# First attention: the query clamp one group later, two masks earlier, and four row maxima moved to another place

## What is computed

```python
x = x + linear_attention(layernorm(x))          # 16 heads of 64, features exp(+f), exp(-f), causal
x = x + cross_attention(layernorm(x), ctx)      # 16 heads of 16, over 1024 context rows
x = x + experts(layernorm(x))                   # 8 experts, the best 2 of each row

def feature_map(t, K):
    f = einsum('hdf,bhld->bhlf', K, t)
    return maximum(concat([softmax(f), softmax(-f)]), 1e-12)
# linear attention: q, k, v = heads(x @ Wq), ...; qf, kf = feature maps
# o_l = sum_{m<=l} (qf_l . kf_m) v_m / (sum_{m<=l} qf_l . kf_m + 1e-12);  then o @ Wo
# cross attention: softmax(q k^T / 4) v, the row maximum subtracted before exp; then @ Wo
```

## Time and profile before

| | |
|---|---|
| time, median of 3 runs | 1252.89 us (1252.18 to 1253.55) |
| the profiled execution | 1252.72 us, its span 1250.9 us |
| busy share of the span | TensorE 92%, VectorE 76%, ScalarE 49%, GpSimd 29% |
| mean granted TensorE clock | 0.973 of full speed |
| first attention | from the start to about 555 us |
| from one L479 to the next over chunk 10 | 360.97 to 391.15 us |

### The profile page before, as it was taken

How to read it: one execution, slowest core, us unless ns; L and a number is a source line. 1 busy time by engine, 2 the same in 40 slices (tenths; PEclk the granted TensorE clock), 3 DMA queues, 4 the chain that set the end, 5 groups by cost and what they waited for, 6 DMA issues and landing times. The chain is left out here.

```text
span 1250.9 us, 29597 instructions
## 1 busy us (share of the span) xinstructions
PE 1147.8 (92%) x11658; PEld 682.9 (55%) x11659; DVE 953.1 (76%) x1758; ACT 610.1 (49%) x1151; POOL 365.3 (29%) x346
## 2 busy tenths in 40 slices
PE   7799899999899999979999999999999847999996
PEld 5566666676667766643344344334434334666665
DVE  6888868887888688778679777877889456677756
ACT  4332333334333333217678776776788722344443
POOL 3322255222522222112310320131100412566651
PEclk9899999999999999999999999999999977999998
DMA  8000025000400000013730480075050161111115
GB/s 255 27 1 2 2 54 104 1 2 1 79 1 2 1 2 1 2 55 58 136 69 9 77 177 4 8 129 102 2 207 2 52 180 41 60 63 63 63 58 204
DMA packets 61928, 73.64 MB, mean 59 GB/s; under 512 B 14336, under 2 KB 53376, under 8 KB 61168
## 3 DMA queue, kind: packets, MB, share of 16 engines
q1 hardware_dynamic: 58016, 61.56, 20.8%
q0 software_dynamic: 3792, 10.36, 2.6%
HBM read 52.86 MB, written 18.78 MB: 57 GB/s over the span
## 5 line engine op out<-in xcount | busy, mean ns | idle before, releaser
L1717 DVE TENSOR_REDUCE neg_max<-pS 128x1 f32<-128x1024 f32 x240 | 287.2, 1220 | 53.5 <-PE pS L1500 53.1
L1632 ACT ACTIVATE pt<-pR 128x512 f32<-128x512 f32 x512 | 286.5, 600 | 80.0 <-PE pR L1523 75.1
L1523 PE MATMUL pR<-qs,ks 100*32 100x512 bf16 x2048 | 190.7, 383 | 1.8 <-ACT pt L1632 1.6
L1500 PE MATMUL pS<-ks,qs 100*32 100x512 bf16 x1920 | 147.3, 382 | 6.0 <-DVE neg_max L1717 2.8
L1537 PE MATMUL b_pO<-pt,b_v 128*32 128x512 f32 x1024 | 135.2, 602 | 2.2 <-ACT pt L1632 1.6
L406 PE MATMUL pP<-w_feat,a_xT 128*128 128x512 f32 x244 | 117.7, 606 | 0.7 <-ACT w_feat L676 0.7
L298 POOL TENSOR_TENSOR kf<-kf,fsum 128x2048 f32<-128x2048 f32 (+1 forms) x17 | 58.1, 3421 | 185.6 <-DVE fsum L867 185.6
L1523 PEld LDWEIGHTS pR<-qs,ks 100*32 100x32 bf16 x2048 | 56.0, 96 | 95.3 <-issue 25.5
L298 POOL TENSOR_TENSOR qs<-qs,fsum 128x2048 f32<-128x2048 f32 (+1 forms) x17 | 58.5, 3446 | 143.4 <-DVE fsum L867 143.4
L1379 POOL COPY qs<-max_rows 3x512 bf16<-3x512 bf16 x60 | 36.7, 611 | 208.9 <-ACT max_rows L1625 205.9
L1500 PEld LDWEIGHTS pS<-ks,qs 100*32 100x32 bf16 x1920 | 51.4, 97 | 76.0 <-issue 35.8
(11 more groups left out here) (339 smaller groups left out, 2124.2 us busy)
## 6 DMA issues: line engine op xcount, KB each, us to landing
ks<-k_scr SPq DMA_DIRECT2D x8, 768.0 KB
qs<-q_scr SPq DMA_DIRECT2D x24, 256.0 KB
k_scr<-f SPq DMA_DIRECT2D x18, 256.0 KB, 2.6
ks<-k_scr SPq DMA_DIRECT2D x8, 512.0 KB
ks<-in_L_ffn_w_dram SPq DMA_DIRECT2D x2, 2048.0 KB, 10.5
ks<-in_L_ffn_w_dram SPq DMA_DIRECT2D x4, 1024.0 KB, 8.7
ks<-y_rows SPq DMA_DIRECT2D x16, 256.0 KB, 5.4
cx<-in_ctx_dram SPq DMA_DIRECT2D x3, 768.0 KB, 12.2
```

What stands on the lines that cost most here:

```text
L1500: ins = pe.matmul(pS1[q:q + XV, slot, 512 * half:512 * half + 512], qs[0:KR, bass.ds(par, 1), h, P * t + q:P * t + q + XV].rearrange("r a ...
L1523: ins = pe.matmul(ring[bank][q:q + XV, :], ks[0:KR, bass.ds(par, 1), h, P * j + q:P * j + q + XV].rearrange("r a n -> r (a n)"), qs[0:KR, ...
L1632: nc.scalar.activation(pt[:, j % 2, i, :], ring[bank], ACT.Exp).then_inc(exp_done, 1)
L1717: nc.vector.tensor_reduce(neg_max[:, hg % 2, u // G, u % G:u % G + 1], pS1[:, u % 2, :], AX_X, ALU.max, negate=True).then_inc(max_done, 1)
```

## The change

Six edits. In the first attention VectorE masks group g + 1 at the head of group g (before, the second query shift and the query sums came first), and clamps the queries of the next chunk in group 3, behind `normalise_o`, instead of in group 2. ScalarE copies the turned features of group 3 before the second query exponential. In chunk 15 `split_max` stands behind `normalise_o` of group 3 instead of ahead of it. Two units of the second head group (16 and 17 in the count of the first attention) are computed there: unit 16's scores before the last `o_transposes`, its maximum behind `split_max`; unit 17's scores inside the last `out_product`, its maximum behind `turned_maxima`. The cross attention starts with units 2 and 3, so that five units instead of seven are left for its opening. For this the table `neg_max` of both head groups is allocated outside the two functions.

```diff
         def unit_scores(u):
-            return pP if u < SOON or u % 2 == 0 else pDW
+            return pP if u < SOON or u % 2 == 0 or u >= NEW else pDW
...
                     for j in range(H // 2):
+                        if t == T - 1 and j == 2:
+                            token_scores(NEW + 1)
                         ins = pe.matmul(y_ps, oT[:, j, :], wo[:, j, :], start=(j == 0), stop=(j == H // 2 - 1))
...
-                    wait(pe, max_done, u if u < SOON else u - 1)
+                    wait(pe, max_done, u if u < SOON else u + 1 if u > NEW else u - 1)
+                    if u >= NEW:
+                        t, h = (u - NEW) // G, G + (u - NEW) % G
...
+                        if final:
+                            token_scores(NEW)
                         o_transposes(t)
...
                         prepare(prep, 2)
+                        prepare(prep, 3)
+                        f_copies(t, 3)
                         if has1:
                             exponentials(1, t + 1, 1, 1 - par)
-                        prepare(prep, 3)
-                        f_copies(t, 3)
...
                         for g in range(G):
+                            if final:
+                                for u in UNITS[g][:2]:
+                                    maximum(u)
+                            if g < G - 1:
+                                mask(t, g + 1)
                             if g == 1 and has1:
                                 shift(1, t + 1, 1, 1 - par, own)
                             if g == 2 and has1:
                                 denominators(1, t + 1, 1 - par, own)
                             if final:
-                                for u in UNITS[g][:2]:
-                                    maximum(u)
-                            if g < G - 1:
-                                mask(t, g + 1)
-                            if final:
                                 for u in UNITS[g][2:3]:
                                     maximum(u)
-                            if final and g == G - 1:
-                                split_max()
                             if g == 0 and has1:
                                 shift(1, t + 1, 0, 1 - par, own)
...
                             normalise_o(t, g, own)
+                            if final and g == G - 1:
+                                split_max()
+                                maximum(NEW)
                             if g == 0 and has2:
                                 normalise(t + 2)
-                            if g == 2 and has1:
+                            if g == G - 1 and has1:
                                 clamp(1, t + 1, 1 - par)
...
                         if final:
                             turned_maxima()
+                            maximum(NEW + 1)
...
-        AHEAD = 2
+        IN_LINEAR, AHEAD = 2, 4
...
-                    U = 16 * (G * b + hg - 1) + u
+                    U = 16 * (G * b + hg - 1) + u - IN_LINEAR
...
-                for u in range(AHEAD):
+                for u in range(IN_LINEAR, AHEAD):
                     scores_by_token(0, 1, u)
```

More of the change, by code:

```diff
@@ L62, in linear_attention @@
 def linear_attention(nc, x, Wq, Wk, Wv, Wo, Kq, Kk, xr, ctx_in, on, Cq, Ck, Cv, k_scr, q_scr, aug_scr,
-                     stats1, mv1, rstd1, q_scale, q_aug, ks, qs, v_first):
+                     stats1, mv1, rstd1, q_scale, q_aug, neg_max, ks, qs, v_first):
     with ExitStack() as ctx:
@@ L129, in linear_attention @@
         cv = ck_raw
-        neg_max = sb("a_neg_max", [P, TB, G])
         max_rest = sb("a_max_rest", [P, TB, G])
@@ L181, in linear_attention @@
         NEW, SOON = 16, 3
+        first_max = neg_max[:, 0]
         UNITS = [range(SOON, SOON + 4), range(SOON + 4, SOON + 8), range(SOON + 8, SOON + 12), range(SOON + 12, NEW)]
         def unit_scores(u):
-            return pP if u < SOON or u % 2 == 0 else pDW
+            return pP if u < SOON or u % 2 == 0 or u >= NEW else pDW
         def prepares(b, c):
@@ L957, in maximum @@
                     dve.wait_ge(s1_done, u + 1)
-                    nc.vector.tensor_reduce(neg_max[:, u // G, u % G:u % G + 1], unit_scores(u)[:, :],
+                    hg, n = u // NEW, u % NEW
+                    nc.vector.tensor_reduce(neg_max[:, hg, n // G, n % G:n % G + 1], unit_scores(u)[:, :],
                                             AX_X, ALU.max, negate=True).then_inc(max_done, 1)
@@ L964, in split_max @@
                     dve.wait_ge(s_k, 14)
-                    rows.did(nc.vector.tensor_copy(max_parts[:, :, :, 0], neg_max[:, :, :]))
+                    rows.did(nc.vector.tensor_copy(max_parts[:, :, :, 0], first_max))
                     rows.wait()
-                    rows.did(nc.vector.tensor_tensor(max_rest[:, :, :], neg_max[:, :, :], max_parts[:, :, :, 0], ALU.subtract))
+                    rows.did(nc.vector.tensor_tensor(max_rest[:, :, :], first_max, max_parts[:, :, :, 0], ALU.subtract))
                     rows.wait()
@@ L1078, in cross_attention @@
 def cross_attention(nc, ctx_in, Wq, Wk, Wv, Wo, k_scr, q_scr, aug_scr, xr, stats, mv, rstd, q_scale, q_aug,
-                    ks, qs, v_first, f, ln_b, f_rows, w1, b1, w1_sb, b1_sb):
+                    neg_max, ks, qs, v_first, f, ln_b, f_rows, w1, b1, w1_sb, b1_sb):
     with ExitStack() as ctx:
@@ L1114, in cross_attention @@
         v1 = sb("b_v1", [P, G, JT, G, XV])
-        neg_max = sb("neg_max", [P, 2, TB, G])
         max_rest = sb("max_rest", [P, TB, G])
@@ L1726, in split_max @@
                 def split_max(b, hg, own, steps):
-                    wait(dve, max_done, 16 * (G * b + hg))
+                    wait(dve, max_done, 16 * (G * b + hg) - IN_LINEAR)
                     wait(dve, filled, steps)
@@ L2546, in decoder_layer @@
         q_scale, q_aug = sb("q_scale", [P, B]), sb("q_aug", [P, L], BF16)
+        neg_max = sb("neg_max", [P, 2, TB, G])
         v_first = ks[:, 1].rearrange("p h n -> p (h n)").bitcast(F32)[:, 4608:6656].rearrange(
@@ L2549, in decoder_layer @@
         linear_attention(nc, x, a_wq, a_wk, a_wv, a_wo, a_kq, a_kk, xr, ctx_in, mask, x_wq, x_wk,
-                         x_wv, k_scr, q_scr, aug_scr, stats, mv, rstd, q_scale, q_aug, ks, qs, v_first)
+                         x_wv, k_scr, q_scr, aug_scr, stats, mv, rstd, q_scale, q_aug, neg_max, ks, qs, v_first)
         w1_sb = ks[:, 0].rearrange("p h n -> p (h n)").bitcast(F32).rearrange("p (e k h) -> p e k h", e=E_, k=KD)
@@ L2555, in decoder_layer @@
         cross_attention(nc, ctx_in, x_wq, x_wk, x_wv, x_wo, k_scr, q_scr, aug_scr, xr, stats, mv, rstd,
-                        q_scale, q_aug, ks, qs, v_first, f, ln_b, f_rows, w1, b1, w1_sb, b1_sb)
+                        q_scale, q_aug, neg_max, ks, qs, v_first, f, ln_b, f_rows, w1, b1, w1_sb, b1_sb)
         experts(nc, gate_w, ln1_g, ln1_b, w2, b2, ln_g, ln_b, f_rows, y_rows, xr, stats, f,
```

2 lines of the change are left out of this document (1 added, 1 removed).

## The result

| | before | changed |
|---|---|---|
| median of 4 runs each | 1253.22 us (1252.18 to 1255.93) | 1237.21 us (1234.88 to 1238.46) |
| the profiled execution, its span | 1252.72, 1250.9 us | 1237.08, 1235.3 us |
| mean granted TensorE clock | 0.973 | 0.982 |

A forecast was written before the change was run, and what follows sets the result against it. A closed VectorE-GpSimd loop of 30.2 us, not TensorE, was taken to bound ordinary chunks. Chunks 10.4 + split 0.8 - unit 17 0.5 + cross-attention opening 2.3 = 13.0 us less, so 1239.9 us; 80% range 1230 to 1251.

The forecast's parts named there:

- the likeliest case: The prediction's own forecast: 1239.9 us, its own range 1234 to 1245, chance 62%.
- The clamp one group later: VectorE, chunk loop: group 3's update and normalisation leave it, -1.08 us; key-projection wait -0.39; mask 1 earlier, -0.24.
- The masks ahead: VectorE, ordinary chunk: mask 3 enters the loop, +0.6 us; mask 2 waits for group 2's scores, +0.62.
- the first rival: The whole gap closes: all 23.9 us of idle time before L479 goes, with the seam 26.5; 1226.4 us; chance 8%.
- the wait of mask 3: VectorE's wait for group 3's scores: nothing added, bounds 0 and another 0.6 us.
- the gap only moves: Rival: TensorE stands at group 3's scores or outputs instead; only 2.6 us gained at the seam, 1250.3 us; chance 15%.
- ScalarE's copies: Group 3's copies before the second query exponential: 0, nobody waits for it; worth 6.2 us at most without TensorE slack.
- The x1 rows: Four VectorE rows in chunk 5, now beside GpSimd's scaling: gain taken as lost, bounds 0 and 1.3 us.
- Unit 17 and the split: End of chunk 15: split of maxima behind normalisation, -0.8 us; unit 17's scores inside the last output product, +0.5.
- The opening of the cross attention: VectorE's start of the cross attention: five maxima instead of seven, 2 x 1.16 = 2.3 us less.
- The signs: L479 idle under 8 us, mostly chunks 14 and 15; loop 29.7; first attention ends 11 earlier; cross attention 2.3 shorter.
- one sign of being wrong: Chunk loop: forecast is wrong if query sums start more than 1 us later against group 1's scores.

The follow-up runs named there:

- masks behind: Changed kernel with masks 2 and 3 back behind the second query shift and the query sums: 1228.71 us, 0.9804.
- seam alone: Kernel before with only the change's end of chunk 15 and its moved units 16 and 17: 1244.76 us, 0.9932.
- masks behind and the x1 rows moved: Changed kernel with masks 2 and 3 back, and chunk 5's four x1 rows moved to group 0 of chunks 6 and 7: 1226.22 us, 0.9789.
- maximum moved: Version with masks back and x1 rows moved, plus unit 0's maximum in chunk 14 ahead of the query clamp: 1226.85 us, 0.9806.
- late clamp and seam alone: Changed kernel with both masks and ScalarE's copies back in their old places: 1227.38 us, 0.9812.

## Why the prediction came true, and by which steps

The direction, the likeliest case and the range held: 1237.2 against 1239.9, in 1230 to 1251. The mechanism held in the main: the late clamp carries the gain (15.0 us with the masks behind, 23 with them ahead), and the masks ahead cost. That the sum came so near is in part luck, as it was made of errors of both signs.

*The clamp one group later.* Right in mechanism and in two of three pieces. The 1.08 and the 0.39 came off. The third, 0.24 at mask 1, did not: mask 0 to mask 1 is 365.90 - 363.89 = 2.01 us, before 2.00. TensorE does stand waiting for mask 0 now (0.35 at 364.73), and group 1's scores take 1.13 from there, ending at 365.86: what is between mask 0's start and the scores' start is 0.84, not mask 0's 0.69. The step took the mask's duration for the delay until its reader starts.

*The masks ahead.* Forecast +0.6 and +0.62, together 1.2 us per ordinary chunk. In the loop of chunk 10 the terms are there, 0.57 of waiting and 0.6 of mask, and with the -0.24 left out the sum is -1.08 - 0.39 + 0.6 + 0.57 = -0.30 of 30.19, the 29.90 that was measured. But taking them back gives only 0.82 per chunk, since at 29.1 us TensorE is the bound, as the first rival had it from the earlier trace rows. In the total it is 8.8 us. The prediction had the sign, and with it that the change holds an edit that loses; it didn't say that the kernel without it would be the faster one. For the wait of mask 3 it kept 0; it is 0 here only because mask 2 has waited before it (0.44 with mask 3 alone ahead).

*The other waits.* Rival "the gap only moves" was half right: of the 23.9 us at L479, 18.8 went, and 8.0 came at L443 and 4.3 at L452, in its mechanism but at other places: group 1's scores for mask 0, and the deltas for the state. To the L479 of chunk 14 the chunks gave 9.45 us where 10.4 were forecast, and some of that is clock: before lost about 1 us to it in chunk 2 (34.49 us, 33.51 in its second profile).

*ScalarE's copies.* Costed at 0 with "nobody waits for it"; bound 6.2. In the changed kernel they are worth 12 us, outside that bound. The step left out that mask 3, moved ahead of the sums in the same change, puts `kfT` of group 3 on the loop (1.08 us of waiting in chunk 10 without the edit). How much of it mask 2 adds, by delaying the shift that the exponential waits for, was not run by itself. The forecast of the whole is untouched by it, since both edits are in.

*The x1 rows.* Taken as 0, bounds 0 and 1.3. Chunk 5 came out 0.3 us longer than before while chunk 10 came out 0.3 shorter. Removing the rows from there gave 1.35, so the hold-up took more than the cover gave. The Trainium skill (SBUF — State Buffer, section "Who interferes with whom") would have the rows start only after the scaling, and so end at 230.52 + 1.38 = 231.90, an estimate. The trace agrees: the first row ends 0.15 us behind the scaling, the last at 231.64.

*Unit 17 and the split.* The split gave 0.9 instead of 0.8. Unit 17 cost 0.86 instead of 0.5 in the changed kernel's profile, but at the lower clock; at the full one it is 0.43, and the term was right.

*The opening of the cross attention.* Forecast 2.3 for two maxima. It gave 3.3 in the changed kernel and 3.1 with the seam alone. The opening took 18.0 to 18.8 us in the four profiles with seven units and 15.1 to 15.4 in the ten with five, so the term was mis-sized by 0.3 to 1.4 us. What makes the difference beyond two maxima was not followed.

*The clock.* Forecast 0 outside the first rival. In the profiles the cross attention behind its opening gave 2.0 us that no term had, most of them clock. Against the forecast the chunks lack 1.0 and unit 17 0.4, the opening gave 1.0 more, the last stage and the residual of chunk 14 0.4 each, the split 0.1: that makes 15.6 of 13.0. Between 60 and 640 us the five profiles with the clamp in its old place have four to seven places of lower clock each, the nine with the late clamp none to three. So the late clamp came with more clock; at which stop the clock falls is not fixed even for one kernel.

*The signs.* L479's idle time came under 8 us, but only 2.1 of the 5.1 lie in chunks 14 and 15. The loop is 29.90 us, forecast 29.7. The first attention ended 9.9 us earlier instead of 11, the cross attention was 5.3 us shorter instead of 2.3. TensorE did not wait at the outputs of group 3. And one sign of being wrong came true: the query sums start 377.02 - 364.73 = 12.29 us behind the scores of group 1, before 382.39 - 371.43 = 10.96, so 1.33 us later where more than 1 was to refute the forecast. The sign was set wrong, for the prediction's own terms for the two masks make 1.2 us of such a delay, and the late clamp pays for it. The query sums of chunk 10 before:

```profile
382.39 2.27 DVE L864 TENSOR_REDUCE fsum<-qs 128x32 f32<-128x2048 f32 x1
```

The version with the masks behind and the x1 rows moved, 0.9789 (0.9773 to 0.9805), beats both the kernel before and the changed one. Its neighbours (masks behind with either order of the copies, and the maximum moved), at 0.9804 to 0.9812, have intervals that overlap its own.

## What to carry to other kernels

When a closed loop between engines sets the pace, move out of it what others wait for late, and put nothing new into it that could stand in a wait's shadow: here late clamp and seam alone gained 7.8 us more than the whole change, and the two masks ahead gave 8.8 us back. Cost an edit against the order that it will stand in, not that of the profile, for one of no worth before can be worth 12 us beside another. Where a stop of TensorE closes, look at the clock of the stretch behind it; the gain can be larger than the stop. But the clock falls at other places from one execution to the next, so before a difference of 2 to 4 us between two profiles is put down to an edit, compare the clock of the same stretch, and take a second profile or the medians.

## What the runs showed of the hardware

- Stops of TensorE of 2.37 us (clamp back in group 2), 2.43 us and 2.50 us (before, 515.81) were followed by a granted clock of 0.72 over 6 us; one of 2.42 us at 238.04 of before was not. The length of the stop doesn't decide alone: the stop of 2.28 us in chunk 2 was followed by 1.00 in one profile of before and by 0.50 over 3 us in the other, and the stops of 0.80 and 1.45 us in chunk 14 by 1.00 in the changed kernel and by 0.72 with mask 3 alone ahead. What else decides was not tried.
- Such a place of lower clock cost 1.7 us where TensorE had no slack: 7.67 against 6.01 us at the end of chunk 15, 9.19 against 7.51 at the end of chunk 14, the same instructions each time.
- Four VectorE rows of 256 elements took 3.88 us beside GpSimd's scaling of 3.62 us, and 1.38 without it. The first of them took 2.91 us, until 0.15 us behind the scaling's end, and the scaling took 3.62 us in both cases.
- The "issue" stop in the cross attention changed its place and its length, 1.9 to 2.3 us in four profiles against 0.8 to 1.5 in ten, when units left the opening ahead of it. Its cause was not shown.
- The last stage, whose code is the same in all kernels, took from 248.0 us (masks behind) to 252.8 (maximum moved) from the last `b_o` to the end, and 250.8 and 249.4 in the two profiles of before. Differences of 1 to 2 us between two profiles' ends are therefore no evidence; medians are, and local rows at the same clock.
